# First layer of the edge network computed in the scatter pass instead of the first gather pass, its activations not stored to DRAM

## The chip, the cores and the metric

The kernel runs on one core of one Trainium2 chip. The metric is device time in microseconds, from the first to the last instruction of one execution. The core has five engines that run their own instruction lists and meet only at semaphores: TensorE (PE), VectorE (DVE), ScalarE (ACT), GpSimd (POOL) and the sync engine (SP), which here only issues transfers.

## The reference

A graph of 12500 nodes with 48 features and 212500 edges, sorted by destination, goes through four message passing blocks, each behind a layer norm and a ReLU. Cut to the second block, which the change concerns:

```python
src, dst = edge_index
gate = silu(edge_attr @ W1.T + b1) @ W2.T + b2           # edge_attr: E x 40, W1: 48 x 40, W2: 48 x 48
adapt_logit = sum(emb[atom_z[src]] * (emb[atom_z[dst]] @ adaptW.T), -1)
gate = gate + adapt_logit
cw = where(distances < CUTOFF, 0.5 * (cos(pi * distances / CUTOFF) + 1), 0)
mj = node_mult[dst]
msg = gate * h[dst] * (cw * mj)[:, None]
agg = segment_sum(msg, src, N);  tot = segment_sum(mj, src, N)
x = layernorm(h + agg / clip(tot, 1e-8)) * gamma + beta
```

The first block is `segment_sum(h[src] * w, dst)`, the third a softmax-weighted sum over `dst`, the fourth two more weighted sums over `dst`.

## The kernel before

Edges are padded to 416 groups (NG) of 4 x 128 edges (G = 4 tiles of P = 128, GW = 512 edges). A turn of a loop is 8 groups (GB), so there are 52 turns. Destinations are sorted, so a group touches one or two windows of 128 destination nodes; the ranges of windows are loaded into registers at the head of each turn (`load_ranges`), and an inner loop runs over them.

The stages run one behind the other, with a barrier between them: setup, the first pass (`first_pass`, L454 to L689), a node stage (L797 to L814), the scatter pass (L833 to L1053), a node stage, then three light passes (`light_pass`) with node stages between them.

First pass, per group: POOL gathers four tiles of source rows by indirect DMA (L476), for which ACT has staged the indices three groups ahead (`stage`, L528). ACT weighs the rows (L545), and ACT and DVE split the product in three bf16 parts (L533, L603, L538, L607). For each window DVE makes `onehot` (L619) and `onet` (L625), PE multiplies them with the parts and with the embedding table (L676, L682), DVE adds the sum (L635), and ACT and DVE keep a running maximum of the logits (L569, L630, L638). PE closes the group with a matmul of zeros (L688), on whose semaphore `s_closed` DVE waits before the four dots (L645). The last dot frees the group (`s_free`): SP then loads the rows of a later group (L506, L507), and ACT stages indices.

Inside this pass the first layer of the edge network rides along: SP loads the 40 x 512 attributes (L502, `attr`), PE multiplies them with `w1s` into `psum_mlp` (L663, at the head of a group and so directly behind the closing matmul of the group before), ACT applies Silu with the bias into `hid` (L584, between `part0` and `part1`), and SP stores `hid` to `hid_dram` (`store_hidden`, L495). The second attribute buffer lies over `same` and the first over `srcrow`, which this pass doesn't use otherwise.

Scatter pass, per group g: SP loads `hid` back (L842) and the broadcast rows (L846, L847). DVE makes `onet` per window (L880) and `same` (L888), PE expands the destination rows with them (L961), closes (L966), runs the second layer of group g+1 (`second_layer`, L934) and then `combine` of group g-1 (L945). ACT forms the gate (L1012), then `part1` of g-1 (L991), `part0` of g (L986) and the hand-over of g-1 to POOL (`hand_over`, L998). DVE makes the rest (L861), the duplicate test (L895), `part2` of g-1 (L865), the product of g (L908), and writes the scatter indices of g (L912), which waits until POOL has issued group g-2. POOL adds the rows of a group into DRAM with four accumulating indirect DMAs (L1045).

Of the kernel before, what the change touches and what calls it, by code (L numbers as in the profile page):

```python
# [6 lines left out]
C = 48  # L7
E = 212500
R = 40
# [9 lines left out]
GB = 2 * RING  # L19
# [30 lines left out]
def gnn_kernel(nc, x, dst_cols, src_cols, dst_rows, src_rows, w_cols, logit_cols, logit_rows,  # L50
# [10 lines left out]
    with ExitStack() as ctx:  # L61
# [15 lines left out]
        hid_dram = dram("hid_dram", (C, NG * GW))  # L77
# [39 lines left out]
        attr = [srcrow[0:R, :, :].rearrange("p r e -> p (r e)").bitcast(f32), same[0:R, :, :, :].rearrange("p r u e -> p (r u e)").bitcast(f32)]  # L117
# [336 lines left out]
        def first_pass(name, src_table, cols, weights):  # L454
# [7 lines left out]
            s_attr = [sem(f"{name}_attr{r}") for r in range(2)]  # L462
            s_mlp1 = sem(name + "_mlp1")
            s_hid = sem(name + "_hid")
            s_hidout = [sem(f"{name}_hidout{r}") for r in range(2)]
            width = src_table.shape[1]
            
            with nc.Block() as block:
# [17 lines left out]
                @block.sync  # L486
                def _(sp):
                    for r in range(2):
                        sp.sem_inc(s_hidout[r], 16)
                    sp.wait_ge(s_zero, 1)  # L490

                    def store_hidden(g, par):
                        sp.wait_ge(s_hid, g + 3)
                        sp.sem_inc(s_seen, 1)
                        sp.dma_start(hid_dram[:, ds(g * GW, GW)], hid[0:C, par, :]).then_inc(s_hidout[par], 16)  # L495

                    def load_pair(i, peeled):
                        for j in range(2):

                            sp.wait_ge(s_mlp1, i * 2 + (j + 1))  # L500
                            sp.sem_inc(s_seen, 1)
# [9 lines left out]
                    load_pair(0, True)  # L511
                    for c in range(K):
                        with sp.Fori(1 + c * CLEARS, 1 + (c + 1) * CLEARS) as i:
                            load_pair(i, False)
                            sp.dma_start(sums[c][ds((i - (1 + c * CLEARS)) * CLEARED, CLEARED), :].rearrange("(p r) c -> p (r c)", p=CLEARED_P),
                                         clear).then_inc(s_cleared, 16)
                    with sp.Fori(1 + K * CLEARS, NG // 2) as i:
                        load_pair(i, False)
                    for g in (NG - 2, NG - 1):
                        store_hidden(g, g % 2)  # L520
                    for r in range(2):
                        sp.wait_ge(s_hidout[r], 16 + 16 * NG // 2)
                    sp.wait_ge(s_cleared, K * CLEARS * 16)

                @block.scalar
                def _(act):
# [26 lines left out]
                    nc.scalar.activation(warm[:, :], b1s[:, :], ACT.Silu)  # L553
                    act.sem_inc(s_hid, 2)
# [3 lines left out]
                    with act.Fori(0, TURNS) as i:  # L558
                        spans = load_ranges(act, i)
                        for j in range(GB):  # L560
                            act.wait_ge(s_bcast[j % 2], i * (16 * GB) + 32 * (j // 2 + 1))
                            act.sem_inc(s_seen, 1)
                            with act.Fori(*spans[j]) as k:
                                win = act.snap(wn_act)

                                act.wait_ge(s_maxed, win)
                                act.sem_inc(s_seen, 1)

                                nc.scalar.activation(pen[:, :], drow[:, j % 2, :], ACT.Abs, scale=BIG, bias=far[:, ds(k, 1)]).then_inc(s_pen, 1)  # L569
# [11 lines left out]
                            act.sem_inc(s_seen, 1)  # L581
                            act.wait_ge(s_hidout[j % 2], i * (8 * GB) + 16 * (j // 2 + 1))
                            act.sem_inc(s_seen, 1)
# [67 lines left out]
                def _(pe):  # L651
                    pe.sem_inc(s_mlp1, 2)
                    pe.reg_mov(wn_pe, 1)
                    with pe.Fori(0, TURNS) as i:
                        spans = load_ranges(pe, i)
                        for j in range(GB):
                            g = i * GB + j

                            pe.wait_ge(s_attr[j % 2], i * (8 * GB) + 16 * (j // 2 + 1))
                            pe.sem_inc(s_seen, 1)  # L660
                            pe.wait_ge(s_hid, g + 1)
                            pe.sem_inc(s_seen, 1)
                            nc.tensor.matmul(psum_mlp[j % 2][0:C, :], w1s[:, :], attr[j % 2], start=True, stop=True).then_inc(s_mlp1, 1)  # L663
# [154 lines left out]
        s_hidin = [sem(f"l1_hidin{r}") for r in range(2)]  # L818
# [14 lines left out]
        with nc.Block() as block:  # L833
            @block.sync
            def _(sp):
                with sp.Fori(0, TURNS) as i:
                    for j in range(GB):
                        g = i * GB + j

                        sp.wait_ge(s_mlp, g + 1)  # L840
                        sp.sem_inc(s_seen, 1)
                        sp.dma_start(hid[0:C, j % 2, :], hid_dram[:, ds(g * GW, GW)]).then_inc(s_hidin[j % 2], 16)  # L842
# [7 lines left out]
                sp.wait_ge(s_mlp, NG + 1)  # L850
                sp.sem_inc(s_hidin[NG % 2], 16)
# [70 lines left out]
            def _(pe):  # L922
                pe.sem_inc(s_mlp, 2)
                pe.reg_mov(wn1_pe, 1)

                def second_layer(i, j):

                    pe.wait_ge(s_hidin[j % 2], i * (8 * GB) + 16 * (j // 2 + 1))
# [20 lines left out]
                def turn(i, peeled):  # L949
                    spans = load_ranges(pe, i)  # L950
                    for j in range(GB):
# [16 lines left out]
                        second_layer(i, j + 1)  # L968
                        if j > 0 or not peeled:
                            combine(g - 1, (j - 1) % 2)  # L970

                second_layer(0, 0)
# [6 lines left out]
            def _(act):  # L979
                act.sem_inc(s_out, 2)  # L980
                act.sem_inc(s_gate, 2)

# [18 lines left out]
                def turn(i, peeled):  # L1001
                    for j in range(GB):
# [11 lines left out]
                        last.then_inc(s_gate, 1)  # L1014
                        if j > 0 or not peeled:
# [4 lines left out]

                turn(0, True)
# [183 lines left out]
```

## Time and profile before

| | us |
|---|---|
| median of 3 runs | 14637.14 |
| lowest, highest | 14630.46, 14647.33 |
| profiled execution | 14613.11 |
| its span | 14611.4 |

Busy time in the profiled execution:

| engine | busy us | share of the span |
|---|---|---|
| PE (matmul) | 6196.8 | 42% |
| PE (weight load) | 4830.5 | 33% |
| DVE | 4470.0 | 31% |
| ACT | 3889.5 | 27% |
| POOL | 9177.6 | 63% |

The granted TensorE clock was 1.0 over the whole span. Busy time counts instructions at work; an engine that is idle may be waiting for another or have nothing to do. The ends of matmuls are modelled, so that a wait behind PE can be longer than the records of PE show; the profile then calls its release "remote". "issue" is idle time for which the profile shows no release.

### The profile page before, as it was taken

The numbers are of one execution on the slowest core, as the hardware profiler recorded it, in microseconds if no ns is written. First come the engines' busy times: TensorE is split into PE (matmuls) and PEld (weight loads), VectorE is DVE, ScalarE is ACT, GpSimd is POOL, SyncE is SP. The second block draws the span as 40 slices with busy tenths as digits, with TensorE's granted clock in tenths as the row PEclk, the third lists the DMA queues.
The fourth block names the chain that finished last, engine by engine and source line by source line (L and its number), as shares of the span: only waits on it lengthen the run. The fifth ranks groups of instructions, "written<-read, shape, count | busy, mean of one in ns | idle before, by whom it ended". The sixth has DMA issues, their size and how long they took to land. (4 is left out here: it accounts for less than half of the span.)

```text
span 14611.4 us, 229268 instructions
## 1 busy us (share of the span) xinstructions
PE 6196.8 (42%) x41742; PEld 4830.5 (33%) x41743; DVE 4470.0 (31%) x18451; ACT 3889.5 (27%) x13481; POOL 9177.6 (63%) x8348
## 2 busy tenths in 40 slices
PE   4444444444555555542333333333333333333333
PEld 2222222223444444432333333233333333333333
DVE  5444444445444444443111111211111121111111
ACT  3444444442333333321111111111111111111111
POOL 5555555556888888874666666566666656666665
DMA  4333333334555555551111111111111111111111
GB/s 117 104 104 102 103 101 102 101 101 57 62 62 61 62 61 61 62 87 35 16 16 16 16 16 16 20 16 16 16 16 16 16 22 16 16 16 16 16 16 21
DMA packets 812412, 690.95 MB, mean 47 GB/s; under 512 B 418932, under 2 KB 671220, under 8 KB 810119
## 3 DMA queue, kind: packets, MB, share of 16 engines
q0 software_dynamic: 452736, 234.14, 14.8%
q1 hardware_dynamic: 357051, 450.30, 11.6%
q10 hardware_dynamic: 2588, 6.12, 0.1%
q14 instruction: 26, 0.21, 0.0%
q8 instruction: 11, 0.18, 0.0%
HBM read 572.77 MB, written 117.06 MB: 47 GB/s over the span
## 5 line engine op out<-in xcount | busy, mean ns | idle before, releaser
L708 POOL DMA_INDIRECT table<-table,idx x4992 | 4822.8, 966 | 3230.0 <-ACT idx L715 1704.7
L786 PE MATMUL psum_acc<-table 128*128 128x48 f32 (+1 forms) x12288 | 2951.1, 417 | 5142.0 <-DVE acc L748 2400.8
L786 PEld LDWEIGHTS psum_acc<-table 128*128 128x128 f32 x12288 | 2734.4, 328 | 5358.7 <-issue 5315.2
L1045 POOL DMA_INDIRECT sums<-rows,idx x1664 | 2621.0, 1575 | 592.8 <-issue 431.5
L476 POOL DMA_INDIRECT rows<-table,idx x1668 | 1673.1, 1003 | 1550.8 <-ACT idx L528 1015.9
L759 DVE TENSOR_TENSOR table<-iota,dstf 128x512 f32 x1536 | 1064.5, 693 | 3025.5 <-issue 2113.7
L715 ACT CAST idx<-srow 128x4 int32 (+1 forms) x1266 | 243.4, 193 | 6334.1 <-DVEq L767 4216.7
L748 DVE TENSOR_TENSOR acc<-acc,psum_acc x1539 | 312.3, 203 | 3467.4 <-remote 2411.0
L961 PE MATMUL psum_exp<-table,onet 128*128 x6144 | 431.4, 219 | 1368.9 <-DVE onet L880 1135.9
L676 PE MATMUL psum_acc<-parts,onehot 128*128 128x48 bf16 x6144 | 338.4, 215 | 1574.5 <-DVE onehot L619 1386.4
L728 ACT ACTIVATE table<-table,w 128x48 f32<-128x48 f32 x3328 | 840.9, 324 | 26.8 <-DMA table<-table,idx 16.8
L961 PEld LDWEIGHTS psum_exp<-table,onet 128*128 128x128 bf16 x6144 | 340.7, 116 | 1502.8 <-issue 1479.9
L934 PE MATMUL psum_mlp<-w2s,hid 49*128 49x48 f32 x3336 | 808.3, 414 | 65.7 <-DMA hid<-hid_dram 65.7
L676 PEld LDWEIGHTS psum_acc<-parts,onehot 128*128 128x128 bf16 x6144 | 271.3, 117 | 1660.9 <-DVE onehot L619 1452.3
L934 PEld LDWEIGHTS psum_mlp<-w2s,hid 49*128 49x128 f32 x3336 | 741.2, 324 | 139.4 <-issue 139.4
L569 ACT ACTIVATE scratch<-drow,far 128x512 f32<-128x512 uint16 x512 | 369.3, 721 | 633.2 <-DVE segmax L638 299.9
L1012 ACT ACTIVATE gate<-psum_mlp,adapt,cw 128x48 f32<-128x48 f32 x1664 | 514.3, 390 | 68.1 <-PE psum_mlp L934 36.2
L991 ACT CAST parts<-rest 128x196 bf16<-128x196 f32 x416 | 150.0, 360 | 1283.3 <-DVE rest L861 864.2
L912 DVE TENSOR_TENSOR idx<-srow,dmp 128x4 int32<-128x4 f32 x416 | 68.7, 165 | 1300.2 <-POOLq L1047 1209.5
L663 PE MATMUL psum_mlp<-srcrow,w1s 40*48 40x512 f32 x416 | 396.9, 1056 | 152.6 <-issue 113.0
L545 ACT ACTIVATE prod<-rows,w 128x48 f32<-128x48 f32 x1668 | 425.2, 324 | 50.7 <-issue 36.8
L728 ACT ACTIVATE table<-table,lg 128x49 f32<-128x49 f32 x1664 | 421.9, 324 | 14.2 <-DMA table<-table,idx 9.0
(171 smaller groups left out, 7187.4 us busy)
## 6 DMA issues: line engine op xcount, KB each, us to landing
drow<-rows_dram SPq DMA_DIRECT2D x832, 128.0 KB
lrow<-in_logit_rows SPq DMA_DIRECT2D x416, 256.0 KB
table<-table,idx POOLq DMA_INDIRECT x4992
srcrow<-rows_dram SPq DMA_DIRECT2D x416, 128.0 KB
hid_dram<-hid SPq DMA_DIRECT2D x416, 96.0 KB
hid<-hid_dram SPq DMA_DIRECT2D x416, 96.0 KB
rows<-table,idx POOLq DMA_INDIRECT x1668
sums<-rows,idx POOLq DMA_INDIRECT x1664
```

What stands on the lines that cost most here:

```text
L476: pool.indirect_dma_start(out=rows[:, u, 0:width], out_offset=None, in_=src_table, in_offset=bass.IndirectOffsetOnAxis(ap=idx[:, u:u + 1], ...
L545: last = nc.scalar.activation(prod[:, j % 2, u, 0:cols], rows[:, j % RING * G + u, 0:cols], ACT.Copy, scale=weights[:, ds(i * U + (j * G + ...
L663: nc.tensor.matmul(psum_mlp[j % 2][0:C, :], w1s[:, :], attr[j % 2], start=True, stop=True).then_inc(s_mlp1, 1)
L676: last = nc.tensor.matmul(psum_acc[:, 0, 0:cols], onehot[:, u, :], parts[:, j % 2, u, q, 0:cols], start=(u == 0 and q == 0), stop=(u == G ...
L708: pool.indirect_dma_start(out=ring[:, u, 0:cols], out_offset=None, in_=src_table, in_offset=bass.IndirectOffsetOnAxis(ap=idx[:, u:u + 1], ...
L728: last = nc.scalar.activation(ring[:, j * G + u, 0:cols], ring[:, j * G + u, 0:cols], ACT.Copy, scale=weights[:, ds(i * U + (j * G + u), 1)])
L759: nv.tensor_tensor(hot[:, j % 2, :, :], iota[:, ds(k * P, P)].unsqueeze(1).to_broadcast([P, G, P]), dstf[:, ds(i * U + j * G, G)].unsqueez ...
L786: last = nc.tensor.matmul(psum_acc[:, ds(win & 1, 1), 0:cols].rearrange("p r c -> p (r c)"), hot[:, j % 2, u, :], ring[:, j * G + u, 0:col ...
L934: last = nc.tensor.matmul(psum_mlp[j % 2][:, u * C:(u + 1) * C], hid[:, j % 2, u * P:(u + 1) * P], w2s[:, :], start=True, stop=True)
L961: last = nc.tensor.matmul(psum_exp[j % 2][:, u * CT:(u + 1) * CT], onet[:, u * P:(u + 1) * P], table[:, ds(k, 1), q, :].rearrange("p b c - ...
L1012: last = nc.scalar.activation(gate[:, j % 2, u, 0:C], psum_mlp[j % 2][:, u * C:(u + 1) * C], ACT.Identity, scale=cw[:, ds(t, 1)], bias=ada ...
L1045: pool.indirect_dma_start(out=sums[c], out_offset=bass.IndirectOffsetOnAxis(ap=idx[:, slot:slot + 1], axis=0), in_=rows[:, slot, 0:CS], in ...
```

## The change

The first layer moves from the first pass to the scatter pass. In the first pass the attribute load, the matmul, the Silu and the store of `hid` go, with their semaphores. In the scatter pass SP loads attributes where it loaded `hid`; PE runs `first_layer` of group g+2 behind `second_layer` of g+1 and ahead of `combine` of g-1, into the two halves of `psum_acc`, free in this pass; ACT runs `hide` of group g+2 behind the gate of g and ahead of `part1` of g-1. `hid` is no longer stored to DRAM, and the attribute buffers lie in `scratch`.

```diff
-        hid_dram = dram("hid_dram", (C, NG * GW))
-        attr = [srcrow[0:R, ...].bitcast(f32), same[0:R, ...].bitcast(f32)]
+        attr = [scratch[0:R, r * GW:(r + 1) * GW] for r in range(2)]
...
# first pass, SP
-                            sp.wait_ge(s_mlp1, i * 2 + (j + 1))
-                            sp.dma_start(attr[j % 2], attr_t[:, ds((i * 2 + j) * GW, GW)]).then_inc(s_attr[j % 2], 16)
...
-                            if j >= 2 or not peeled:
-                                store_hidden(i * 2 + (j - 2), j % 2)
# first pass, ACT
-                            act.wait_ge(s_mlp1, i * GB + (j + 3))
-                            act.wait_ge(s_hidout[j % 2], i * (8 * GB) + 16 * (j // 2 + 1))
-                            nc.scalar.activation(hid[0:C, j % 2, :], psum_mlp[j % 2][0:C, :], ACT.Silu,
-                                                 bias=b1s[:, 0:1]).then_inc(s_hid, 1)
# first pass, PE
-                            pe.wait_ge(s_attr[j % 2], i * (8 * GB) + 16 * (j // 2 + 1))
-                            pe.wait_ge(s_hid, g + 1)
-                            nc.tensor.matmul(psum_mlp[j % 2][0:C, :], w1s[:, :], attr[j % 2], start=True, stop=True).then_inc(s_mlp1, 1)
...
# scatter pass, SP
-                        sp.wait_ge(s_mlp, g + 1)
+                        sp.wait_ge(s_first, g + 1)
-                        sp.dma_start(hid[0:C, j % 2, :], hid_dram[:, ds(g * GW, GW)]).then_inc(s_hidin[j % 2], 16)
+                        sp.dma_start(attr[j % 2], attr_t[:, ds(g * GW, GW)]).then_inc(s_attr[j % 2], 16)
# scatter pass, PE
+                def first_layer(i, j):
+                    pe.wait_ge(s_attr[j % 2], i * (8 * GB) + 16 * (j // 2 + 1))
+                    pe.wait_ge(s_hid, i * GB + (j + 1))
+                    nc.tensor.matmul(psum_acc[0:C, j % 2, :], w1s[:, :], attr[j % 2], start=True, stop=True).then_inc(s_first, 1)
                 def second_layer(i, j):
-                    pe.wait_ge(s_hidin[j % 2], i * (8 * GB) + 16 * (j // 2 + 1))
+                    pe.wait_ge(s_hid, i * GB + (j + 3))
...
                         second_layer(i, j + 1)
+                        first_layer(i, j + 2)
                         if j > 0 or not peeled:
                             combine(g - 1, (j - 1) % 2)
# scatter pass, ACT
+                def hide(g, par):
+                    act.wait_ge(s_first, g + 3)
+                    act.wait_ge(s_mlp, g + 1)
+                    nc.scalar.activation(hid[0:C, par, :], psum_acc[0:C, par, :], ACT.Silu, bias=b1s[:, 0:1]).then_inc(s_hid, 1)
...
                         last.then_inc(s_gate, 1)
+                        hide(g + 2, j % 2)
                         if j > 0 or not peeled:
                             part1(g - 1, (j - 1) % 2)
```

## Rows read from the trace of the kernel before

**Rows 1.** Stages: stretch, length, busy us (count) by engine, PEclk, DMA share, GB/s
```profile
133.00:3327.00 3194.00, 1502.47 (x13952) 660.70 (x13950) 1411.58 (x7225) 1410.68 (x4260) 1666.64 (x1662) 1.00 0.39 102
3390.00:6530.00 3140.00, 1697.27 (x15304) 1392.08 (x15304) 1378.69 (x8000) 948.29 (x2912) 2620.80 (x1664) 1.00 0.52 61
6680.00:9280.00 2600.00, 975.72 (x4054) 901.82 (x4055) 446.87 (x1017) 497.87 (x2065) 1603.75 (x1664) 1.00 0.12 16
```

**Rows 2.** Costliest groups: busy, mean ns | idle before; POOL in the scatter pass
```profile
L1045 POOL DMA_INDIRECT sums<-rows,idx x1664 | 2621.0, 1575 | 592.8 <-issue 431.5 <-ACT rows L998 92.3 <-DMA sums<-rows,idx 45.6
```

**Rows 3.** Timeline, scatter pass: start, length, what [idle before <-releaser]
```profile
4773.31 1.56 POOL L1045 DMA_INDIRECT sums<-rows,idx  x1 [0.30 <-issue]
...
4775.02 0.16 DVE L912 TENSOR_TENSOR idx<-srow,dmp 128x4 int32<-128x4 f32 x1 [5.51 <-POOLq L1047]
4775.61 0.35 DVE L880 TENSOR_SCALAR onet<-drow,node 128x512 bf16<-128x512 uint16 x1 [0.43 <-issue]
...
4776.88 0.34 PE L966 MATMUL psum_exp<-zeros 1*128 1x200 bf16 x1
...
4777.15 1.94 PE L934 MATMUL psum_mlp<-w2s,hid 49*128 49x48 f32 x8
4777.15 0.36 ACT L991 CAST parts<-rest 128x196 bf16<-128x196 f32 x1 [4.81 <-DVE rest L861]
...
4777.80 0.35 DVE L865 TENSOR_TENSOR parts<-rest,parts 128x196 bf16<-128x196 f32 x1
...
4778.35 0.36 DVE L908 TENSOR_TENSOR prod<-gate,psum_exp 128x196 f32<-128x196 f32 x1
4778.82 0.36 ACT L986 CAST parts<-prod 128x196 bf16<-128x196 f32 x1 [1.32 <-DVE prod L908]
...
4780.19 0.27 SPq L842 DMA_DIRECT2D hid<-hid_dram  x1
4780.21 1.24 ACT L1012 ACTIVATE gate<-psum_mlp,adapt,cw 128x48 f32<-128x48 f32 x4
...
4781.66 0.35 DVE L880 TENSOR_SCALAR onet<-drow,node 128x512 bf16<-128x512 uint16 x1 [0.35 <-issue]
...
4783.23 0.62 DVE L880 TENSOR_SCALAR onet<-drow,node 128x512 bf16<-128x512 uint16 x1 [1.22 <-issue]
```

**Rows 4.** Timeline of POOL in the first pass
```profile
2502.66 1.09 POOL L476 DMA_INDIRECT rows<-table,idx  x1 [4.51 <-ACT idx L528]
...
2519.06 0.94 POOL L476 DMA_INDIRECT rows<-table,idx  x1 [5.33 <-ACT idx L528]
```

**Rows 5.** Groups of instructions of the first pass
```profile
L584 ACT ACTIVATE hid<-psum_mlp,b1s 48x512 f32<-48x512 f32 x416 | 282.9, 680 | 57.0 <-issue 56.3 <-remote 0.5
...
L645 DVE CUSTOM_DVE_ANT_0 dots<-rows,psum_exp 128x32 f32<-128x32 f32 x1664 | 212.1, 183 | 681.4 <-remote 626.5 <-issue 47.4 <-PE psum_exp L688 7.6
...
L635 DVE TENSOR_TENSOR acc<-acc,psum_acc 128x48 f32 x512 | 104.9, 205 | 876.8 <-remote 811.8 <-PE psum_acc L676 38.9 <-issue 2.5
```

**Rows 6.** Timeline of one group's end in the first pass
```profile
2503.38 1.91 PE L663 MATMUL psum_mlp<-srcrow,w1s 40*48 40x512 f32 x2
...
2506.91 0.19 DVE L645 CUSTOM_DVE_ANT_0 dots<-rows,psum_exp 128x32 f32<-128x32 f32 x1 [3.13 <-remote]
```

**Rows 7.** Timeline of the light pass, inside an unbroken run of gathers
```profile
8012.94 0.21 DVE L748 TENSOR_TENSOR acc<-acc,psum_acc  x1 [7.28 <-remote]
```

**Rows 8.** Timeline, scatter pass, first group of a turn
```profile
5003.84 0.35 DVE L880 TENSOR_SCALAR onet<-drow,node 128x512 bf16<-128x512 uint16 x1 [2.52 <-issue]
```

**Rows 9.** Timeline, start of the scatter pass: first transfers and their first users
```profile
3389.88 0.33 SPq L842 DMA_DIRECT2D hid<-hid_dram  x1
...
3391.03 0.34 SPq L847 DMA_DIRECT2D srcrow<-rows_dram  x1
...
3392.24 1.91 PE L934 MATMUL psum_mlp<-w2s,hid 49*128 49x48 f32 x8 [65.74 <-DMA hid<-hid_dram]
...
3394.70 0.35 DVE L880 TENSOR_SCALAR onet<-drow,node 128x512 bf16<-128x512 uint16 x1 [5.71 <-DMA srcrow<-rows_dram]
```

More of the change, by code:

```diff
@@ L115, in gnn_kernel @@
         lrow = sb("lrow", [P, 2, GW])
-        attr = [srcrow[0:R, :, :].rearrange("p r e -> p (r e)").bitcast(f32), same[0:R, :, :, :].rearrange("p r u e -> p (r u e)").bitcast(f32)]
+        attr = [scratch[0:R, r * GW:(r + 1) * GW] for r in range(2)]
         hid = sb("hid", [C + 1, 2, GW])
@@ L461, in first_pass @@
             s_bcast = [sem(f"{name}_bcast{r}") for r in range(2)]
[L462 to L465, printed above, removed]
             width = src_table.shape[1]
@@ L487, in _, with load_pair @@
                 def _(sp):
-                    for r in range(2):
-                        sp.sem_inc(s_hidout[r], 16)
                     sp.wait_ge(s_zero, 1)
[L492 to L497, printed above, removed]
+                    def load_pair(i):
                         for j in range(2):
-                            sp.wait_ge(s_mlp1, i * 2 + (j + 1))
-                            sp.sem_inc(s_seen, 1)
-                            sp.dma_start(attr[j % 2], attr_t[:, ds((i * 2 + j) * GW, GW)]).then_inc(s_attr[j % 2], 16)
                             sp.wait_ge(s_free, i * 2 + (j + RING - 1))
@@ L507, in load_pair @@
                             sp.dma_start(lrow[:, j % 2, :], logit_rows[ds(i * 2 + j, 1), :].squeeze(0).partition_broadcast(P)).then_inc(s_bcast[j % 2], 16)
-                            if j >= 2 or not peeled:
-                                store_hidden(i * 2 + (j - 2), j % 2)
-                    load_pair(0, True)
+                    load_pair(0)
                     for c in range(K):
                         with sp.Fori(1 + c * CLEARS, 1 + (c + 1) * CLEARS) as i:
-                            load_pair(i, False)
+                            load_pair(i)
                             sp.dma_start(sums[c][ds((i - (1 + c * CLEARS)) * CLEARED, CLEARED), :].rearrange("(p r) c -> p (r c)", p=CLEARED_P),
@@ L517, in _ @@
                     with sp.Fori(1 + K * CLEARS, NG // 2) as i:
[L518 to L522, printed above, removed]
+                        load_pair(i)
                     sp.wait_ge(s_cleared, K * CLEARS * 16)
@@ L551, in _ @@
                     weigh(0, 0)
-                    nc.scalar.activation(warm[:, :], b1s[:, :], ACT.Silu)
-                    act.sem_inc(s_hid, 2)
                     part0(0, 0)
@@ L651, in _ @@
                 def _(pe):
-                    pe.sem_inc(s_mlp1, 2)
                     pe.reg_mov(wn_pe, 1)
@@ L817, in gnn_kernel @@
         s_in = [sem(f"l1_in{r}") for r in range(2)]
-        s_hidin = [sem(f"l1_hidin{r}") for r in range(2)]
+        s_attr = [sem(f"l1_attr{r}") for r in range(2)]
+        s_first = sem("l1_first"); s_hid = sem("l1_hid")
         s_same = sem("l1_same"); s_dup = sem("l1_dup"); s_dmp = sem("l1_dmp"); s_idx1 = sem("l1_idx")
@@ L847, in _ @@
                         sp.dma_start(srcrow[:, j % 2, :], rows16_dram[1, ds(g, 1), :].squeeze(0).partition_broadcast(P)).then_inc(s_in[j % 2], 16)
-                sp.wait_ge(s_mlp, NG + 1)
-                sp.sem_inc(s_hidin[NG % 2], 16)
+                for g in (NG, NG + 1):
+                    sp.wait_ge(s_first, g + 1)
+                    sp.sem_inc(s_seen, 1)
+                    sp.sem_inc(s_attr[g % 2], 16)
             @block.vector
@@ L923, in _ @@
                 pe.sem_inc(s_mlp, 2)
+                pe.sem_inc(s_first, 2)
                 pe.reg_mov(wn1_pe, 1)
+                def first_layer(i, j):
+                    pe.wait_ge(s_attr[j % 2], i * (8 * GB) + 16 * (j // 2 + 1))
+                    pe.sem_inc(s_seen, 1)
+                    pe.wait_ge(s_hid, i * GB + (j + 1))
+                    pe.sem_inc(s_seen, 1)
+                    nc.tensor.matmul(psum_acc[0:C, j % 2, :], w1s[:, :], attr[j % 2], start=True, stop=True).then_inc(s_first, 1)
                 def second_layer(i, j):
-                    pe.wait_ge(s_hidin[j % 2], i * (8 * GB) + 16 * (j // 2 + 1))
+                    pe.wait_ge(s_hid, i * GB + (j + 3))
                     pe.sem_inc(s_seen, 1)
@@ L968, in turn @@
                         second_layer(i, j + 1)
+                        first_layer(i, j + 2)
                         if j > 0 or not peeled:
                             combine(g - 1, (j - 1) % 2)
+                first_layer(0, 0)
+                first_layer(0, 1)
                 second_layer(0, 0)
@@ L981, in _ @@
                 act.sem_inc(s_gate, 2)
+                act.sem_inc(s_hid, 2)
+                def hide(g, par):
+                    act.wait_ge(s_first, g + 3)
+                    act.sem_inc(s_seen, 1)
+                    act.wait_ge(s_mlp, g + 1)
+                    act.sem_inc(s_seen, 1)
+                    nc.scalar.activation(hid[0:C, par, :], psum_acc[0:C, par, :], ACT.Silu, bias=b1s[:, 0:1]).then_inc(s_hid, 1)
                 def part0(g, par):
@@ L1019, in turn @@
                             hand_over(g - 1, (j - 1) % RING)
+                hide(0, 0)
+                hide(1, 1)
                 turn(0, True)
```

4 lines of the change are left out of this document (removed).

## The prediction

> **What bounds the kernel now.** Three views, in this order. First the busy time by stage, because shares of the whole span mix five loops. The change touches two stages, each over 416 groups of 512 edges: the first pass (133 to 3327 us), 3194/416 = 7.68 us a group, and the scatter pass (3390 to 6530 us), 3140/416 = 7.55. The light passes behind them are not edited; one stands beside them for comparison, 2600/416 = 6.25 [rows 1]. Then, in each stage, the waits and the order of single groups.
>
> The scatter pass is bound by POOL: four indirect DMAs a group, 1.56 us each with 0.30 between them, 7.45 us, and with the longer ones (mean 1575 ns) 7.5 [rows 2, 3]. The others wait for it: DVE stood idle for 5.51 us before it could write the next indices at 4775.02, released by POOL's sequencer [rows 3]. So a group's work on the other engines has slack. Under that cover the change puts its work, and its size decides.
>
> The first pass is bound by no single engine. POOL needs 5.0 us a group (four times 0.94 and the same 0.30) but stands idle in between, here 4.51 and 5.33 us, until ACT has staged indices [rows 4]. DVE is idle for 681 us ahead of the dots and 877 us ahead of the accumulation, mostly until a release that the profile calls remote [rows 5]. One group shows it: the first layer's two passes (L663) follow PE's closing matmul (L688) at 2503.38 and last 1.91 us; DVE, which needs only the closing matmul, began its dots at 2506.91 after 3.13 us of idle [rows 6]. Two things can be in that wait: L663, directly behind the closing matmul, and a hold that the gathers put on the other engines. The second exists without L663: in the light pass, without first layer or SP transfers, DVE stood idle 7.28 us for PE while POOL issued gather after gather [rows 7].
>
> **First pass: what goes.** Per group one fp32 matmul (1.91 us on PE), one Silu on ACT (0.68 us) [rows 5, 6], and on SP the attr load and the hidden store with their waits. PE and ACT have idle time, so their busy time is worth nothing by itself. What counts is that DVE's release no longer stands behind L663. Bounds: nothing is gained if the gathers hold it anyway; with POOL always fed a group takes 5.0 us and 416 x 2.68 = 1115 us go. Between them: dots that come 1 to 2 us earlier let the next indices be staged before a run of four gathers (5 us) ends, so runs become 8 or 12. The pause behind a run stays; I take 4.6 [rows 4]. Runs of 8: (10.1 + 4.6)/2 = 7.35 us a group; runs of 12: (15.0 + 4.6)/3 = 6.5. The light pass, which has nothing of L663, makes 6.25 [rows 1]. I take 6.8, near the middle: 416 x 0.88 = 366 us gained, between 133 (7.36) and 532 (6.4). SP's shorter list lies in this range; it helps the broadcasts for which ACT waits.
>
> The Trainium skill (SBUF — State Buffer, section "SBUF: two separate sides") says that DMA ports and engine ports are disjoint and that PE and ACT wait for nobody there. By that rule gathers cannot hold PE, and the first pass would fall to 5.0 us a group, 749 us more than my term gives. The light pass speaks against it: POOL needs 5.0 us there too, and it takes 6.25 [rows 1, 7].
>
> **Scatter pass: what comes.** The hidden load becomes the attr load at the same place in SP's list: no more issues, and 80 KB for 96. PE gets the 1.91 us matmul behind second_layer and ahead of combine. ACT gets the 0.68 us Silu (hide) behind the gate and ahead of part1, and hide waits for that matmul. Queued behind this wait on ACT are part1, part0 and the hand-over to POOL; DVE's part2, and behind it the product and the next index write, wait for part1. So the new work is in series with DVE's loop. A group with one window, from its start at the index write [rows 3]: onet +0.59, closing matmul +1.27, second layer +0.27, together 2.13. Its 1.94 less 0.07 of overlap: 4.00. First layer 1.91: 5.91. Signal 0.11, hide 0.68: 6.70. Part1 0.36 less 0.10 (four gates of 0.39 take 1.24): 6.96. Signal 0.11: part2 starts at 7.07, where today it starts at 2.78 (4777.80). Product +0.55, 7.62; next index write +0.26, 7.88. That is over POOL's 7.5. Today it is 2.78 + 0.81 = 3.6, with 3.9 of slack.
>
> The slack also hid two things that now count. A group whose destinations span two windows (512 windows in 416 groups, so 96) takes 1.57 us more, 4781.66 to 4783.23 [rows 3, 5]. The first group of each of the 52 turns starts its onet after 2.52 us of idle instead of 0.43, 2.1 more [rows 3, 8]. Mean of the loop: 7.88 + 96/416 x 1.57 + 52/416 x 2.1 = 8.5.
>
> POOL makes it longer. It starts group n when n-1 is issued and the hand-over of n is done, and DVE writes the indices of n when POOL has issued n-2. The hand-over ends at 7.62 + 0.36 (product) + 0.11 + 0.36 (part0) + about 0.26 = 8.7. Two groups thus take at least 8.7 + 7.5, or 8.1 each even with one window. Stepping both rules by arithmetic through the groups, second windows and turn starts where the trace has them, gives 8.79, since a long group delays both; the same steps with today's chain give 7.56, where the trace has 7.55.
>
> Last, the attr load. SP issues it 1.48 us after the product's end (4778.71 to 4780.19) [rows 3]; its matmul could start 7.88 + 4.00 - 7.98 = 3.9 us after it. No row shows a landing under load: a hidden load landed within 2.36 us at the quiet start (3389.88 to 3392.24), a broadcast within 3.67 (3391.03 to 3394.70) [rows 9]. The first costs nothing; the second 1.3 us in each short group, which steps to 9.4. I take 2.95, near the middle: 8.95. Cost 416 x (8.95 - 7.55) = 582 us, between 516 (8.79) and 770 (9.4). Silu's one table load moves with it.
>
> **Sum.** -366 + 582 = +216. The profiled execution took 14613.1 us: 14829. The median of the runs is 24 us above it: 14853.
>
> **Rivals.** (a) Faster: without L663 POOL is fed nearly without pause, 5.0 to 6.3 us a group. It decides below 6.28, where the gain passes 582. At 5.7 the gain is 824: 14637 - 242 = 14395. For it: some 1500 us of DVE idle there [rows 5]. Against it: the light pass [rows 7]. (b) Much slower: the fp32 matmul holds PE longer than its modelled 1.91; from its start to DVE's release 3.5 us passed [rows 6]. With 1.6 more in the scatter chain the steps give 10.1: +1060 - 366, 15331. Against it: the second layer, fp32 too, delays nobody today. (c) The cover holds and the scatter pass stays at 7.55: 14271. It needs a part1 that doesn't wait for hide, and ACT's order excludes that.
>
> **How the numbers follow.** Forecast 0.56, (a) 0.25, (b) 0.16, (c) 0.03. The forecast's own range is 14621 (-532 + 516) to 15274 (-133 + 770). A measurement can tell about 0.2%, 29 us, from no change. Faster: most of (a), (c), a little of the forecast, 0.28; same 0.06; slower 0.66. The range 14300 to 15350 leaves out the fastest third of (a), the slower half of (b), and (c), together just under 0.2.
>
> **What would show it.** First pass: near 2830 us, POOL in runs of 8 and 12 gathers, no 3 us waits ahead of the dots. Scatter pass: near 3720 us; index writes that wait little for POOL, part1 behind hide, POOL idle until the hand-over. If POOL keeps 1.86 us from start to start there, my chain is wrong; if the first pass stays over 3060 us, the gathers' hold took the gain.

## The result

The changed kernel takes 15235.1 us (median of 4 runs, 15222.01 to 15248.89) where the kernel before, timed beside it, takes 14636.3 (14630.46 to 14647.33): ratio 1.041, 95% interval 1.0393 to 1.0426. It is 599 us slower; the prediction was 216 us slower. The kernel got slower, as forecast, and the scatter pass got longer in the way that was told; the gain in the first pass did not come at all.

The busy time by stage of the changed kernel, which answers to [rows 1] (stretch, length, busy us and count of PE, PEld, DVE, ACT and POOL, PEclk, DMA share, GB/s):

```profile
133.00:3328.00 3195.00, 680.91 (x13068) 540.02 (x13068) 1410.47 (x7190) 1147.89 (x3826) 1651.36 (x1662) 1.00 0.32 79
3421.00:7156.00 3735.00, 2498.55 (x16061) 1484.31 (x16058) 1344.41 (x7959) 1176.16 (x3313) 2605.75 (x1664) 1.00 0.42 49
7306.00:9886.00 2580.00, 971.95 (x4048) 899.97 (x4048) 443.91 (x1013) 495.44 (x2055) 1608.25 (x1664) 1.00 0.12 16
```

The first pass is as long as before although PE lost 822 us of work in it and ACT 263. From POOL's first gather to its last it takes 7.69 us a group; measured in the same way it took 7.66 before. The scatter pass takes 8.98 us a group, 7.52 before: 416 x 1.46 = 607 us, the whole loss. The light pass didn't change.

The costliest groups that matter (line, engine, tiles, count | busy, mean ns | idle before, releasers), first pass first:

```profile
L471 POOL DMA_INDIRECT rows<-table,idx x1668 | 1657.7, 994 | 1577.4 <-ACT idx L505 1105.9 <-issue 471.5
L613 DVE CUSTOM_DVE_ANT_0 dots<-rows,psum_exp 128x32 f32<-128x32 f32 x1664 | 211.9, 182 | 341.6 <-remote 267.7 <-PE psum_exp L649 61.0 <-issue 12.9
L603 DVE TENSOR_TENSOR acc<-acc,psum_acc 128x48 f32 x512 | 104.8, 205 | 1195.7 <-remote 1152.2 <-PE psum_acc L637 22.1
...
L1034 POOL DMA_INDIRECT sums<-rows,idx x1664 | 2605.7, 1566 | 1222.0 <-ACT rows L984 813.7 <-issue 408.2
L898 PE MATMUL psum_acc<-scratch,w1s 40*48 40x512 f32 x836 | 801.3, 1060 | 343.4 <-DMA scratch<-in_attr_t 341.7 <-issue 1.4
L967 ACT ACTIVATE hid<-psum_acc,b1s 48x512 f32<-48x512 f32 x418 | 285.1, 682 | 2109.7 <-PE psum_acc L898 2109.7
L829 DVE TENSOR_TENSOR parts<-rest,parts 128x196 bf16<-128x196 f32 x416 | 151.3, 364 | 2060.2 <-ACT parts L977 2060.2
L876 DVE TENSOR_TENSOR idx<-srow,dmp 128x4 int32<-128x4 f32 x416 | 63.7, 153 | 0.0
```

Read the first three lines against [rows 5]. The idle time ahead of the dots fell from 681.4 to 341.6 us, that ahead of the accumulation rose from 876.8 to 1195.7. Together 1558 before and 1537 after: DVE waits as long, only more of it at the accumulation and less at the dots. POOL's gathers waited as long before as after (1577.4 above):

```profile
L476 POOL DMA_INDIRECT rows<-table,idx x1668 | 1673.1, 1003 | 1550.8 <-ACT idx L528 1015.9 <-issue 534.9
```

In the scatter pass the index write (L876), which stood idle for POOL 5.51 us in the group of [rows 3], never waits now. DVE waits for part1 (L977), ACT for the first layer (L898), and POOL, the bound before, waits for the handed-over rows (L984): 1222 us idle where it was 593 [rows 2].

One loop of DVE in the scatter pass, with one window, from index write to index write (start us, length, instruction, idle before and its releaser):

```profile
5010.51 0.15 DVE L876 TENSOR_TENSOR idx<-srow,dmp 128x4 int32<-128x4 f32 x1
...
5012.27 0.31 SPq L804 DMA_DIRECT2D scratch<-in_attr_t  x1
5012.35 1.68 POOL L1034 DMA_INDIRECT sums<-rows,idx  x1 [1.30 <-ACT rows L984]
...
5012.41 1.94 PE L908 MATMUL psum_mlp<-w2s,hid 49*128 49x48 f32 x8
...
5015.27 1.91 PE L898 MATMUL psum_acc<-scratch,w1s 40*48 40x512 f32 x2 [0.93 <-DMA scratch<-in_attr_t]
...
5017.41 0.68 ACT L967 ACTIVATE hid<-psum_acc,b1s 48x512 f32<-48x512 f32 x1 [4.80 <-PE psum_acc L898]
5017.99 0.34 ACT L977 CAST parts<-rest 128x196 bf16<-128x196 f32 x1
...
5018.37 0.36 DVE L829 TENSOR_TENSOR parts<-rest,parts 128x196 bf16<-128x196 f32 x1 [5.13 <-ACT parts L977]
...
5018.85 0.35 DVE L872 TENSOR_TENSOR prod<-gate,psum_exp 128x196 f32<-128x196 f32 x1
...
5019.12 0.15 DVE L876 TENSOR_TENSOR idx<-srow,dmp 128x4 int32<-128x4 f32 x1
```

This is the series of the prediction: second layer, first layer, hide, part1, part2, product, index write. Before the change part2 ran 2.78 us after the index write, here 7.86. The first layer waits 0.93 us for its attributes.

### The profile page after: what moved, and what is told of

It reads as the page before. It is cut to its first block and busy times, and to the rows that moved or that the text cites. A ratio compares the mean times of both kernels' runs of the same rounds, so it can differ in the third digit from the quotient of the medians.

```text
span 15224.7 us, 225703 instructions
## 1 busy us (share of the span) xinstructions
PE 6198.1 (41%) x41746; PEld 4812.3 (32%) x41747; DVE 4445.4 (29%) x18451; ACT 3868.5 (25%) x13483; POOL 9152.9 (60%) x8348
## 5 line engine op out<-in xcount | busy, mean ns | idle before, releaser
L471 POOL DMA_INDIRECT rows<-table,idx x1668 | 1657.7, 994 | 1577.4 <-ACT idx L505 1105.9
L898 PE MATMUL psum_acc<-scratch,w1s 40*48 40x512 f32 x836 | 801.3, 1060 | 343.4 <-DMA scratch<-in_attr_t 341.7
L967 ACT ACTIVATE hid<-psum_acc,b1s 48x512 f32<-48x512 f32 x418 | 285.1, 682 | 2109.7 <-PE psum_acc L898 2109.7
L829 DVE TENSOR_TENSOR parts<-rest,parts 128x196 bf16<-128x196 f32 x416 | 151.3, 364 | 2060.2 <-ACT parts L977 2060.2
L919 PEld LDWEIGHTS psum_comb<-parts,same 128*128 128x128 bf16 x4992 | 229.9, 117 | 1402.9 <-issue 1402.9
L919 PE MATMUL psum_comb<-parts,same 128*128 128x49 bf16 x4992 | 274.2, 217 | 706.8 <-DVE parts L829 706.8
L515 ACT CAST parts<-rest 128x192 bf16<-128x192 f32 x417 | 147.7, 354 | 1348.1 <-DVE rest L571 1140.4
```

Source lines behind the costliest of these rows:

```text
L471: pool.indirect_dma_start(out=rows[:, u, 0:width], out_offset=None, in_=src_table, in_offset=bass.IndirectOffsetOnAxis(ap=idx[:, u:u + 1], ...
L898: nc.tensor.matmul(psum_acc[0:C, j % 2, :], w1s[:, :], attr[j % 2], start=True, stop=True).then_inc(s_first, 1)
L919: last = nc.tensor.matmul(psum_comb[par][:, u * CS:(u + 1) * CS], same[:, par, u, :], parts[:, par, u, q, :], start=(q == 0), stop=(q == P ...
```

## The experiments

The runs came in six sets on several chips. The same kernel before takes 14636 us in the set of the result, 14700 in one more, and 12122 to 12134 in the other four, which fell on three chips. So each experiment is compared with what ran beside it, or by its stages. The stage times are taken from POOL's first to its last gather or scatter, divided by 416 groups. "The hold" is the prediction's word: while POOL issues gathers, other engines wait long for releases. The sets of 14636 and 14700 us show it, the other four don't; the part on the first pass has the evidence.

**The chain in the scatter pass.** First the order alone is changed: both new pieces of work go behind what DVE waits for.

```diff
-                        first_layer(i, j + 2)
                         if j > 0 or not peeled:
                             combine(g - 1, (j - 1) % 2)
+                        first_layer(i, j + 2)
...
-                        hide(g + 2, j % 2)
...
                             hand_over(g - 1, (j - 1) % RING)
+                        hide(g + 2, j % 2)
```

> The changed kernel with only the order altered in the scatter pass: PE runs first_layer behind combine, ACT runs hide behind the hand-over. Work, transfers and semaphores stay. My theory (the new matmul and Silu cost because they stand in DVE's loop, ahead of part1): the scatter pass returns to POOL's 7.5 us a group, from 8.98, so 15235 - 607 = about 14630 us, within 40. Rival (the added work itself, or the landing of the attributes, costs wherever it stands): the pass stays near 8.9 and the kernel near 15200 us.

Measured: 12149.2 us, ratio to the kernel before on that chip 1.0021 (1.0012 to 1.0031); the scatter pass 7.53 us a group. The absolute times that I expected were those of the other chip; the pass is what counts. Its lines in this kernel:

```profile
L1034 POOL DMA_INDIRECT sums<-rows,idx x1664 | 2626.3, 1578 | 596.9 <-issue 434.5 <-ACT rows L984 96.7 <-DMA sums<-rows,idx 49.3
L829 DVE TENSOR_TENSOR parts<-rest,parts 128x196 bf16<-128x196 f32 x416 | 149.8, 360 | 164.5 <-ACT parts L977 164.2
L876 DVE TENSOR_TENSOR idx<-srow,dmp 128x4 int32<-128x4 f32 x416 | 68.4, 164 | 1136.2 <-POOLq L1036 1135.3
```

POOL's idle time is back at 597 us (593 in [rows 2]), and the index write waits for POOL again. The added matmul, Silu and transfers cost next to nothing once they stand outside the loop: 27 us, 0.2%, in all. Moving hide alone tells which of the two places matters.

> The changed kernel with one move: ACT runs hide behind the hand-over; PE still runs first_layer ahead of combine. Theory (what costs is that part1, and behind it DVE's part2, product and index write, queue behind ACT's wait for the first layer): DVE's chain is free again, combine and the hand-over come at most 1.9 us later beside POOL's work, and the scatter pass takes 7.5 to 7.9 us a group, from 8.95: about 12150 to 12320 us where the changed kernel takes 12751. Rival (the first layer's place on PE, ahead of combine, delays the hand-over for which POOL waits): over 8.3 us a group, over 12480 us.

Measured: 12153.8 us beside 12121.8, one run each; the pass 7.51 us a group. ACT's place is the one that costs: part1 must not stand behind the wait for the first layer. PE's place ahead of combine is free as long as ACT's is right. Both reordered kernels ran on chips without the hold only.

The changed kernel, unaltered, on the chip of the first set, with the kernel before as a second trace:

> The changed kernel itself, unaltered, beside the kernel before on the chip of this set. The first four experiments ran where the kernel before took 12122 us, not 14636, with light passes at 5.1 us a group instead of 6.25. If this set runs there too: both scatter passes keep their length (7.52 and 8.97 us a group), so the change costs 600 us by itself; theory (both first passes are bound by POOL there, 5.3 us a group): 12122 + 607 = 12730 us, ratio 1.05. Rival (without the hold the first layer stood in the way in the kernel before, and its going is a gain): up to 0.88 us a group less, 12122 + 607 - 366 = 12363 us. If this set runs where the kernel before takes 14636 us: 15235 again.

Measured: 12751.0 us, ratio 1.0509 (1.0492 to 1.0527). Scatter pass 8.95 us a group, first pass 5.32. The theory's 12730 is 21 us off, the rival's 12363 is out.

Next the size of the terms. With the matmul issued twice:

```diff
+                    nc.tensor.matmul(psum_acc[0:C, j % 2, :], w1s[:, :], attr[j % 2], start=True, stop=True)
                     nc.tensor.matmul(psum_acc[0:C, j % 2, :], w1s[:, :], attr[j % 2], start=True, stop=True).then_inc(s_first, 1)
```

> The changed kernel with the first layer's matmul in the scatter pass issued twice into the same place, so 1.9 us more on PE ahead of hide. Theory (the matmul is in series with the loop over part1, part2, product, next index write and onet): the pass takes 1.6 to 1.9 us a group more than 8.95, 665 to 790 us, about 13480 us where the changed kernel takes 12751. Rival (other waits, such as the landing of the attributes or the hand-over, set the loop, and the matmul runs beside them): less than 0.8 us a group more, under 13090 us.

Measured: 13433.9 us; the pass 10.58 us a group, 1.63 more than 8.95. So 85% of the 1.91 us come through: the matmul is in series. Why 0.28 us are missing isn't known. (The two kernels ran on different chips, both without the hold.)

With the attributes loaded two groups earlier, into four buffers:

```diff
-                        sp.dma_start(attr[j % 2], attr_t[:, ds(g * GW, GW)]).then_inc(s_attr[j % 2], 16)
+                        sp.dma_start(attr[(j + 2) % 4], attr_t[:, ds((g + 2) * GW, GW)]).then_inc(s_attr[(j + 2) % 4], 16)
```

> The changed kernel with the attributes of group g+2 loaded at step g into four buffers, two groups earlier; order of the work as in the change. In the trace of the changed kernel PE stands idle 342 us for the attributes ahead of the first layer. If these waits are in the series chain, as the prediction's step from 8.79 to 8.95 us a group has it, the kernel gets 60 to 150 us faster, to about 15130 us. Rival (the attribute wait only overlaps other waits): 15235 us, within 30.

Measured: 12502.6 us where the changed kernel takes 12751 on the same chip: 248 us, more than either theory said. The pass falls from 8.95 to 8.36 us a group. The loop of this kernel, same columns as above:

```profile
4005.49 0.16 DVE L879 TENSOR_TENSOR idx<-srow,dmp 128x4 int32<-128x4 f32 x1
...
4009.51 1.94 PE L901 MATMUL psum_acc<-scratch,w1s 40*48 40x512 f32 x2
4011.67 0.68 ACT L970 ACTIVATE hid<-psum_acc,b1s 48x512 f32<-48x512 f32 x1 [4.08 <-PE psum_acc L901]
4012.26 0.35 ACT L980 CAST parts<-rest 128x196 bf16<-128x196 f32 x1
4012.63 0.36 DVE L832 TENSOR_TENSOR parts<-rest,parts 128x196 bf16<-128x196 f32 x1 [4.39 <-ACT parts L980]
4013.11 0.35 DVE L875 TENSOR_TENSOR prod<-gate,psum_exp 128x196 f32<-128x196 f32 x1
...
4013.38 0.16 DVE L879 TENSOR_TENSOR idx<-srow,dmp 128x4 int32<-128x4 f32 x1
```

Here the loop is the bare chain. Over the 276 groups with one window that don't open a turn it is 7.71 us long (mean) and part2 starts 6.96 us in; the prediction had 7.88 and 7.07. Two windows take 9.33 (1.62 more; predicted 1.57), the first of a turn 9.94 (2.2 more; predicted 2.1). In the changed kernel the three are 8.66, 9.26 and 9.95: only the short groups lose by the wait for attributes.

**The first pass.** The kernel before on the chip without the long waits:

> The kernel before itself, for its trace on this chip. If the chip is the one of the first four experiments: theory (POOL sets the first pass as soon as nothing holds the other engines, first layer there or not): first pass at 5.2 to 5.5 us a group, within 0.15 of the changed kernel, and the dots and the accumulation with no idle time behind PE. Rival (the first layer's matmul was a wait of its own): 6 us a group or more. On the other chip: 7.65 us a group as before.

Measured: 12131.0 us. Stages, and the groups of the first pass:

```profile
125.00:2339.00 2214.00, 1497.89 (x13926) 658.66 (x13926) 1445.95 (x7209) 1364.00 (x4251) 1692.78 (x1668) 1.00 0.55 148
2424.00:5553.00 3129.00, 1688.15 (x15227) 1384.01 (x15226) 1368.40 (x7958) 944.26 (x2897) 2622.66 (x1664) 1.00 0.50 61
5702.00:7806.00 2104.00, 987.34 (x4088) 909.95 (x4088) 455.19 (x1025) 481.86 (x2076) 1597.11 (x1664) 1.00 0.13 20
```

```profile
L476 POOL DMA_INDIRECT rows<-table,idx x1668 | 1693.5, 1015 | 553.5 <-issue 467.5 <-ACT idx L528 86.0
L645 DVE CUSTOM_DVE_ANT_0 dots<-rows,psum_exp 128x32 f32<-128x32 f32 x1664 | 209.6, 181 | 0.0
L635 DVE TENSOR_TENSOR acc<-acc,psum_acc 128x48 f32 x512 | 104.8, 205 | 33.3 <-PE psum_acc L676 8.0
```

The same code, the same busy times per instruction, and no wait behind PE: 681 and 877 us of idle time [rows 5] have become 0 and 33. POOL is fed nearly always; it waits for ACT's indices 86 us in all, not for 4 to 5 us between runs [rows 4]. The release itself shows that the first layer's matmul, which stands behind the closing matmul here too, doesn't delay the dots: the semaphore of L688 goes up 0.30 us after that matmul starts, in all 356 groups where the trace has it. In the kernel before of the first set the same release came 3.8 us (median) after the start. The pass takes 5.31 us a group, and 5.32 in the changed kernel beside it: of this 5.2 is POOL's own (1693.5 us busy and 467.5 of "issue"). The light passes are at 5.06 to 5.07, not 6.25, and the scatter pass of the kernel before at 7.52 in every trace. What differs between the chips is the hold that the prediction saw in the light pass [rows 7], and it is in the passes that gather.

Now the gathers themselves: one a group in place of four, in the changed kernel and in the kernel before.

```diff
-                        for u in range(j % RING * G, (j % RING + 1) * G):
+                        for u in range(j % RING * G, j % RING * G + 1):
                             pool.indirect_dma_start(
```

> The changed kernel with one gather a group in the first pass in place of four (three of four tiles of rows keep the value 1; all other work stays). Theory (the gathers hold the other engines, and that hold sets the first pass with or without the first layer): POOL needs 1.24 us a group and no run of gathers is longer than 1 us, so the 3 us waits ahead of the dots go and the pass falls from 7.68 to 4.5 to 6 us a group, 14500 to 14000 us in all. Rival (the pass is set by something that has nothing to do with the gathers, such as the broadcasts on SP's list or the chain from the parts over PE to the accumulation): it stays over 7 us a group.

> The kernel before with one gather a group in the first pass in place of four: the first layer still rides along there. Theory (in the full kernels the gathers' hold covers the first layer's matmul, which is why taking it away brought nothing): with the hold gone the matmul's 1.9 us stands in the way of the dots, and this first pass takes 0.5 to 1.9 us a group more than that of the changed kernel with one gather, 200 to 790 us. Rival (the matmul was never ahead of the dots, hold or not): both first passes are equal within 0.2 us a group.

Measured, on the chip without the hold: 12406.7 and 11821.9 us in all, first passes (first line without the first layer, second with it) of 4.53 and 4.60 us a group.

```profile
125.00:2012.00 1887.00, 678.77 (x13069) 538.61 (x13069) 1435.50 (x7203) 1116.07 (x3828) 413.61 (x417) 1.00 0.39 106
```

```profile
125.00:2039.00 1914.00, 1487.99 (x13897) 654.74 (x13898) 1435.45 (x7199) 1346.74 (x4244) 413.03 (x417) 1.00 0.50 144
```

With POOL out of the way 0.8 us a group of the pass go, and the first layer's matmul is worth 0.07 us, not the 0.5 to 1.9 of my theory. The rival is right: this matmul was not ahead of the dots, hold or not. These two runs say nothing of the hold, because this chip doesn't have it. Their scatter passes, 8.97 and 7.52 us a group, repeat the full kernels'.

The opposite edit, the first layer's matmul issued twice in the kernel before, was run with four gathers a group and with one. This set fell on a chip where the kernel before takes 14700 us.

> The kernel before with the first layer's matmul in the first pass issued twice into the same place, 1.9 us a group more on PE behind the closing matmul. Theory (in the first pass this matmul sets nothing: POOL does where the kernel before takes 12122 us, the hold on the releases where it takes 14636): the pass stays within 0.15 us a group of its length without the doubling (5.31 or 7.65), the kernel within 60 us. Rival (the matmul delays the dots and so the next indices, as my prediction had it): 0.5 to 1.9 us a group more, 200 to 790 us.

> The kernel before with one gather a group in the first pass in place of four (three tiles of rows keep the value 1) and with the first layer's matmul issued twice. With one matmul this pass took 4.60 us a group, without any 4.53, DVE being busy for about 3.4 of it. Theory (DVE and ACT in turn set this pass, and PE works on the first layer while DVE makes the next group's one-hots): one more matmul costs under 0.5 us a group. Rival (PE is close to being the bound: with POOL out of the way 1.9 us more come through): over 1 us a group, over 400 us.

Measured: 14735.8 us beside 14700.4, one run each, so 35 us for 416 x 1.9 = 790 us of added PE work. That is within the 60 us that I allowed. The pass takes 7.85 us a group; its length without the doubling is known only from the first set (7.66), and 0.19 over that is a little more than the 0.15 allowed. With one gather the kernel takes 13820.6 us, the pass 5.69 us a group. First the doubled kernel with four gathers, then the one with one:

```profile
L476 POOL DMA_INDIRECT rows<-table,idx x1668 | 1677.7, 1006 | 1623.6 <-ACT idx L528 1086.7 <-issue 536.9
L645 DVE CUSTOM_DVE_ANT_0 dots<-rows,psum_exp 128x32 f32<-128x32 f32 x1664 | 212.4, 184 | 782.6 <-remote 742.6 <-issue 36.6 <-PE psum_exp L689 3.3
L635 DVE TENSOR_TENSOR acc<-acc,psum_acc 128x48 f32 x512 | 104.7, 204 | 864.9 <-remote 783.3 <-PE psum_acc L677 48.1 <-issue 10.6
```

```profile
L646 DVE CUSTOM_DVE_ANT_0 dots<-rows,psum_exp 128x32 f32<-128x32 f32 x1664 | 210.9, 183 | 33.8 <-PE psum_exp L690 33.8
L636 DVE TENSOR_TENSOR acc<-acc,psum_acc 128x48 f32 x512 | 104.7, 205 | 660.0 <-PE psum_acc L678 653.1
```

On one chip, between two kernels that differ in the number of gathers alone, 742.6 + 783.3 us of "remote" waits become none. So the gathers make the hold. Nor is it the load on the DMA engines: the pass with one gather moved 116 GB/s at a DMA share of 0.41 (row below), the doubled kernel with four gathers 100 at 0.38, with the hold. In the same execution the light passes, with their four gathers a group, still take 6.25 to 6.27 us a group. Whether the number of gathers or the length of their runs makes it, this pair doesn't tell. What is left, 660 us ahead of the accumulation, is a wait for matmuls that the trace shows. The second expectation missed: 5.69 us against 4.60 with one matmul (on another chip) is 1.1 us more.

```profile
125.00:2498.00 2373.00, 2140.70 (x14721) 796.05 (x14722) 1422.24 (x7191) 1386.66 (x4243) 442.07 (x417) 1.00 0.41 116
```

PE is busy 2140.7 us of this pass's 2373, 5.1 us a group, so with two matmuls PE itself is probably the bound. That is argued from the busy time: the kernel with one gather and one matmul wasn't run on this chip.

Last in this part, a pause: POOL waits, ahead of each group's gathers, for the landing of the group before.

```diff
+                        if j > 0:
+                            pool.wait_ge(s_rows[(j - 1) % RING], i * (GB // RING * 16 * G) + ((j - 1) // RING + 1) * 16 * G)
```

> The changed kernel; in the first pass POOL waits, ahead of each group of four gathers, until the rows of the group before have landed, so that no run of gathers is longer than 5 us. POOL then needs 5.0 us and a pause of 1 to 1.5 us a group, 6.0 to 6.5. Where the kernel before takes 14636 us, theory (the hold sets in some us into an unbroken run of gathers and ends with it): the first pass falls from 7.68 to 6.2 to 6.8 us a group, 400 to 600 us less. Rival (the hold depends on the gathers in flight or on their number, not on unbroken runs): 7.6 us a group or more. Where it takes 12122 us nothing is there to be broken, and the pause costs 0.7 to 1.2 us a group, about 400 us more.

```profile
L476 POOL DMA_INDIRECT rows<-table,idx x1668 | 1717.2, 1030 | 1499.0 <-DMA rows<-table,idx 1059.5 <-issue 407.5 <-ACT idx L512 32.0
```

Measured: 13712.8 us on the chip without the hold, the first pass 7.63 us a group, 2.3 more. The pause is 2.5 us (1059.5/416), twice what I expected. It shows the price of waiting for a gather to land. Whether a pause would break the hold stays open: it wasn't tried where the hold is.

**A version to beat both.** Both moves and the early attributes together:

> The changed kernel with first_layer behind combine, hide behind the hand-over, and the attributes loaded two groups earlier into four buffers. Theory (POOL's scatters set this pass once the first layer is out of DVE's loop, and POOL or the hold sets the first pass): neither pass gets shorter than in the kernel before, 7.5 us a group and 5.3 or 7.65; ratio to the kernel before 1.000 to 1.003. Rival (the lighter first pass, with 41 MB less written and 41 MB less read in all, is worth something once the scatter pass is repaired): ratio under 0.998.

Measured: 12147.8 us, ratio 1.0020 (1.0011 to 1.0030), on a further chip without the hold; passes of 5.32 and 7.53 us a group. No version beat the kernel before. The repaired kernels read and write 41 MB less each (572.8 to 531.9 and 117.1 to 76.2 MB) and win nothing, because POOL sets both passes on these chips. With the hold no repaired kernel was run. Its first pass is that of the changed kernel, which took 7.69 us a group there for 7.66, so no gain is in sight; that is argued and not measured.

## Why the prediction was right or wrong

**What bounds the scatter pass: right.** POOL at 7.5 us a group, with slack under it. It is 7.51 to 7.53 in every trace where the new work is absent (with the hold or without) or stands outside DVE's loop (run without the hold only).

**The series chain: right, with its sizes.** 7.88 us predicted for a short group, 7.71 measured when nothing else waits; the second window and the turn start within 0.1. Weighted as in the prediction this gave 8.5; the kernel with early attributes has 8.36.

**The step that couples the loop with POOL: wrong.** I let DVE write the indices of group n when POOL's records show n-2 done, and by that raised 8.5 to 8.79. The changed kernel's index write never waits. The trace of before had the answer: in 340 of 404 groups the index write of group g starts when the last scatter begun is the second of group g-3. The wait (L912) asks for group g-2 to be issued, whose last scatter is six behind. So POOL's sequencer runs six scatters ahead of the records of its engine, some 11 us, and its release comes that much earlier than I took it. The Trainium skill (Advanced Engine Details and Errata, section "Engine Queue Depths") gives GpSimd a queue of 8 instructions, and six lie within it. But the trace shows another limit, in the code: ahead of each scatter the sequencer waits until the scatter eight before it, the last one into the same of the eight `sums`, has landed (L1044). In 1177 of the 1656 such waits of the kernel before it went on within 0.1 us of that landing. So the lead of six is mostly the code's own wait, and no run here shows a full queue.

**The landing of the attributes: right in kind, too small.** I took 2.95 us after issue, between 2.36 and 3.67, and by the coupled steps +0.16 us a group. The runs give 8.95 - 8.36 = 0.59. In the changed kernel 284 groups wait for their attributes; in them the first layer starts 3.1 us (median, mean 3.3) after the issue, and PE would have been ready after 2.3. So the landing was taken only 0.35 us too short. The rest is the coupling again: without it my own 2.95 us makes a short group late by 1.48 + 2.95 - 3.9 = 0.53 us, and two thirds of the groups are short, 0.35 us a group and not 0.16. The errors cancel, 0.43 too much by the coupling (8.79 for 8.36) and 0.43 too little behind it (0.16 for 0.59): 8.95 predicted, 8.98 and 8.95 measured. The hit of the sum is luck in these two terms.

**The first pass: wrong, and all of the miss.** The term was -366 us. The stage measured the other way by 416 x 0.03 = 11 us. Two sentences failed. "What counts is that DVE's release no longer stands behind L663": without the hold it never stood behind it (0.30 us from the start of the closing matmul to its release, L663 or not), and removing L663 moves the pass by 0.01 us a group with four gathers and by 0.07 with one. Under the hold the closing matmul's release comes 3.8 us after its start with L663, 3.1 without and 3.9 with it doubled (medians), but the pass doesn't follow: the doubling costs 35 us, a twentieth of its busy time. Why the release comes 0.7 us earlier without L663 stays open. And "dots that come 1 to 2 us earlier let the next indices be staged": they came earlier (340 us less idle ahead of them), but the accumulation waited 319 us more, so POOL's wait for indices stayed (1551 us idle before, 1577 after). The step from this to runs of 8 or 12 gathers failed on its start too: the runs weren't of four. Between the two pauses of [rows 4] lie eight gathers, with 1.18 us in their middle:

```profile
2506.57 0.94 POOL L476 DMA_INDIRECT rows<-table,idx  x1 [0.30 <-issue]
2508.69 1.29 POOL L476 DMA_INDIRECT rows<-table,idx  x1 [1.18 <-issue]
...
2512.78 0.94 POOL L476 DMA_INDIRECT rows<-table,idx  x1 [0.30 <-issue]
```

Parted at pauses of over 3 us, 165 of 197 runs in the kernel before are of 8, and 178 of 209 in the changed one. Runs of four with a pause of 4.6 would be 9.6 us a group where the trace has 7.66; runs of 8 gave 7.35 by my own sum. So the model's first step, from runs of 4 to runs of 8, had been taken before the change.

The bound below, "nothing is gained if the gathers hold it anyway", was written down as an end of the term and then left out of the range of the term, 133 to 532. With 0 for it the same sum gives 14613 + 582 + 24 = 15219, 16 us from the result.

**The rivals.** (a), POOL fed without pause, is refuted with the hold and without: with it the pass stays at 7.69, and without it POOL was fed already in the kernel before. The rule of the Trainium skill (SBUF — State Buffer, section "SBUF: two separate sides") by which DMA and PE can't contend for ports, read as in the prediction, agrees with the sets of 12122 to 12134 us and not with those of 14636 and 14700. There PE's releases came late while POOL gathered; whether a port has to do with it no run shows. (b), more time in the matmul than its 1.91, is refuted by the chain (7.71). (c) fell as said; moving hide made its scatter half true, 7.51 us a group, and its first-pass half doesn't exist.

## What to carry to other kernels

Where work moves into a stage with slack, find the loop that hides under the bound and put the work behind that loop's waits, on every engine that waits for it: one line's order on ACT was worth 600 us here. Where an instruction stands in front of an unexplained ("remote") wait, look whether the same wait exists where the instruction doesn't; if it does, its removal is worth zero until shown, and the term's likely value is that end. When two queued engines are stepped, take the release of a sequencer from where the trace shows it, not from the end of the engine's record. And before runs are made longer on paper, count how long they are.

## What the hardware showed that I had not expected

The same kernel takes 12122 to 12134 us in four sets and 14636 and 14700 us in two, and the difference is in the passes that gather: a light pass takes 5.1 or 6.25 us a group, the first pass 5.3 or 7.66, the scatter pass 7.52 on both. The gathers take as long in each (1003 and 1015 ns). In the slower sets the release of PE's closing matmul comes 3.8 us (median) after its start where it takes 0.30 in the faster ones; whether the matmul or its signal is late the records don't tell. Other engines' sequencers are held too: between 300 and 1900 us, 222 of 2928 of SP's instructions other than transfers took over 0.5 us (median 0.03) in the kernel before, 246 of 2859 with the matmul doubled, and on that same chip with one gather a group none of 3923; in the faster sets none of 4209. Accumulating scatters make next to no such hold: 7 of 1231 between 4000 and 5000 us. What distinguishes the chips the runs don't show, nor whether the two slower sets ran on the same one.

The price of the change is nearly the same in time: 599 us of 14636 (4.1%) with the hold, 617 of 12134 (5.1%) without.
